# Probabilities over A's rows turned by a crossbar transpose, as two float16 pieces, ahead of the product with A

## The reference, cut to what matters

```python
xn = layernorm(x)                                   # x: (16, 512, 256) float32
# attention: 16 heads of 16, one key and value head for all
q = (xn @ Wq.T + bq) / 4 ; k, v = split(xn @ Wkv.T + bkv)
o = softmax(q k^T) v ; attn = o @ Wo.T + bo
# mixture over E = 6 experts, each with L = 100 low-rank tokens (A: 6x100x16, B: 6x16x256)
gates = one_hot(argmax(xn @ w_gate))                # TOP_K = 1: the chosen gate is 1
tokens = A @ B
p = softmax(xn . tokens / sqrt(C))                  # over the 100 rows of A, per expert
val = tokens @ wt_w.T + wt_b
delta_f = p[:, 1:] @ val[1:]                        # row 0 is left out
delta = ((delta_f + xn) @ wd_w.T + wd_b) * scale
out = x + attn + xn + log(sum_e gates_e * exp(delta_e))
```

## Time and profile before

| what | us |
|---|---|
| median of 3 runs | 902.43 (899.44 to 903.38) |
| the profiled execution, its own time | 902.32 |
| its span, first to last instruction | 900.4 |
| TensorE busy | 857.9 |
| VectorE busy | 780.2 |
| ScalarE busy | 674.6 |
| GpSimd busy | 512.7 |

### The profile page before, as it was taken

The page is one execution under the profiler, slowest core; times in us unless marked ns, Lnnn a source line. Parts: engine busy times, 40 slices in busy tenths (PEclk is TensorE's granted clock), DMA queues, the critical chain, the costliest instruction groups (busy, mean ns, idle before and its releaser), DMA issues.

```text
span 900.4 us, 17856 instructions
## 1 busy us (share of the span) xinstructions
PE 857.9 (95%) x5913; PEld 288.0 (32%) x5913; DVE 780.2 (87%) x1489; ACT 674.6 (75%) x1370; POOL 512.7 (57%) x691
## 2 busy tenths in 40 slices
...
DMA packets 125073, 86.06 MB, mean 96 GB/s; under 512 B 57143, under 2 KB 109112, under 8 KB 124984
## 3 DMA queue, kind: packets, MB, share of 16 engines
q1 hardware_dynamic: 124824, 84.82, 38.2%
q10 hardware_dynamic: 160, 0.10, 0.0%
...
## 4 chain that ended last, share of the span: by engine, by line
PE 79%; DVE 15%; issue 3%; ACT 1%; POOL 1%; DMA 1%; SPq 0%; DVEq 0%
PE pO L373 25%; PE pA L355 19%; DVE M L829 9%; PE pB L360 8%; PE pA L496 5%; PE pA L443 5%; PE pA L514 4%; PE pA L498 3%; PE pA L432 2%; PE pA L468 2%; PE pA L483 2%; DVE st L749 2%; PE pB L476 1%; ACT P L648 1%; PE pB L454 1%
## 5 line engine op out<-in xcount | busy, mean ns | idle before, releaser
L829 DVE TENSOR_REDUCE M<-pA 128x1 f32<-128x512 f32 x1024 | 651.9, 681 | 80.1 <-PE pA L355 76.0
L648 ACT ACTIVATE P<-pB 128x512 f32<-128x512 f32 x1002 | 555.4, 603 | 133.2 <-PE pB L360 129.6
L355 PE MATMUL pA<-K,Q 48*128 48x512 f16 x1024 | 324.6, 388 | 25.1 <-DVE M L829 9.8
L360 PE MATMUL pB<-Q,K 50*128 50x512 f16 x1002 | 317.5, 385 | 0.3 <-DVE M L829 0.3
L373 PE MATMUL pO<-P,VK 128*32 128x512 f32 x2048 | 273.5, 606 | 2.1 <-ACT OTr L654 1.1
L355 PEld LDWEIGHTS pA<-K,Q 48*128 48x128 f16 x1024 | 67.8, 94 | 344.7 <-DVE M L829 285.1
L975 POOL TENSOR_SCALAR Cz<-Cx 128x512 f32<-128x512 f32 x32 | 62.1, 1941 | 38.6 <-ACT Cx L630 38.6
L373 PEld LDWEIGHTS pO<-P,VK 128*32 128x32 f32 x2048 | 40.5, 108 | 99.2 <-issue 66.2
L514 PE MATMUL pA<-wo,On 128*128 128x256 f32 x246 | 70.2, 407 | 0.0
L360 PEld LDWEIGHTS pB<-Q,K 50*128 50x128 f16 x1002 | 64.0, 94 | 7.4 <-ACT P L648 5.5
L960 POOL TENSOR_SCALAR Ms<-M 128x32 f32<-128x32 f32 x32 | 9.7, 303 | 97.5 <-DVE M L829 97.5
...
## 6 DMA issues: line engine op xcount, KB each, us to landing
o_parts<-OTr SPq DMA_DIRECT2D x62, 256.0 KB, 2.3
...
out<-OUT SPq DMA_DIRECT2D x32, 256.0 KB, 3.4
Op<-o_parts SPq DMA_DIRECT2D x31, 256.0 KB
Rb<-l_parts SPq DMA_DIRECT2D x31, 256.0 KB
Q<-q_pieces SPq DMA_DIRECT2D x30, 256.0 KB, 4.5
...
```

Of the source, the lines that this page charges most:

```text
L355: e.matmul(bank1("ab", t)[:, :], Q16[r:r + 48, b % 3, h, 128 * s:128 * s + 128], K16[r:r + 48, b % 3, :], start=True, stop=True).then_inc( ...
L360: e.matmul(bankB(t)[:, :], K16[r:r + 50, b % 3, 128 * i:128 * i + 128], Q16[r:r + 50, b % 3, :, 32 * hh:32 * hh + 32], start=True, stop=Tr ...
L648: e.activation(P[:, u % PR, :], bankB(u + LB)[:, :], ACT.Exp, scale=alpha).then_inc(S("e"))
L829: e.tensor_reduce(M[:, t // 32 % 2, t % 2, t % 32 // 2:t % 32 // 2 + 1], bank1("ab", t)[:, :], AX, ALU.max, negate=True).then_inc(S("mx"))
```

## The change

- The float32 transposes "p" on TensorE and the copy "pte" on ScalarE go. GpSimd, behind En in "snorm", writes En as two float16 pieces (a cast, then a subtraction) into EP, 128 x 2 x 4 x 128 with zeros in the last 28 columns of each block.
- A new step "pd" at 51 modulo 64 on SyncE's queue: one crossbar transpose of EP, 8 blocks of 128x128, into PT. It waits for the low piece and for the product of the batch before.
- "a" becomes three float16 matmuls of 512 columns over the pieces of A and of the probabilities. A's pieces are made once, in the new step "ams" on GpSimd, scaled by the power of two of the weights; A counts in that power, so it is loaded early, from ScalarE's queue, and its maximum joins the setup of VectorE.
- The sums of the softmax are scaled by 2^-11 ahead of the reciprocal (one more VectorE operation of 128x4 per batch); "mm" takes the scale back through a scalar operand.
- Order: "a" moves from 59 to 63 modulo 64, d0 from 63 to 3, d1 from 3 to 7; o0 moves from 7 to 31, o1 from 31 to 35, o2 from 35 to 51 (a batch's o0 is at 159 in place of 135, o2 at 179 in place of 163); position 59 of TensorE is empty. guard0, dlog0, radd0, residual, qs0, qw0, ks, kd, qs1, qw1, guard1, dlog1, radd1 and the second half's lr, or, rec, lw, rb, on move later by 1.2 to 5 tiles. The second lr and or now stand behind pd (52.8 and 52.9 against 51), and the second rb (62.4) behind xtd (61.8).

The diff, cut to its core (fac gains an eighth factor, 2^-33 times the weights' power, copied with the others):

```diff
@@ -38,20 +38,20 @@
 SLOT = {
     "load": -116, "stats0": -97, "stats1": -96, "stats2": -95, "stats3": -94, "aggr": -93, "var": -92.4,
     "root": -91.4, "refine": -90.2, "norm": -87.2, "ph": -82.4, "pl": -79, "xtd": -66.2,
-    "residual": 9.1, "q0": -53, "qe0": -51.4, "qs0": -47.5, "qw0": -45, "uk": -49, "uke": -47.4, "ks": -45.2,
-    "kd": -42.6, "vg": -45, "vge": -44.3, "q1": -41, "qe1": -39.4, "qs1": -38.2, "qw1": -35.6,
+    "residual": 12.8, "q0": -53, "qe0": -51.4, "qs0": -43.8, "qw0": -41.4, "uk": -49, "uke": -47.4, "ks": -41.5,
+    "kd": -38.8, "vg": -45, "vge": -44.3, "q1": -41, "qe1": -39.4, "qs1": -37, "qw1": -34.4,
     "vt": -37, "vte": -36.4, "gate": -34.8, "mask": -32.6, "mkd": -31.4,
     "qread": -25.8, "utm": -24.9, "s": -21,
-    "smax": -20.4, "sexp": -18.8, "ssum": -17.4, "snorm": -16.2, "p": -13, "pte": -12.4, "a": -5, "mm": -4.4,
-    "d0": -1, "dexp0": -0.4, "d1": 3, "dexp1": 3.6, "guard0": 4.8, "dlog0": 9.4, "radd0": 14.8,
-    "d2": 39, "dexp2": 39.6, "d3": 47, "dexp3": 47.6, "guard1": 51.7, "dlog1": 56.2, "radd1": 57.6,
-    "o0": 135, "fo0": 135.6, "o1": 159, "fo1": 159.6, "st0": 163.2, "o2": 163, "fo2": 163.6, "o3": 183,
+    "smax": -20.4, "sexp": -18.8, "ssum": -17.4, "snorm": -16.2, "pd": -13, "a": -1, "mm": -0.4,
+    "d0": 3, "dexp0": 3.6, "d1": 7, "dexp1": 7.6, "guard0": 8.8, "dlog0": 14.2, "radd0": 18.5,
+    "d2": 39, "dexp2": 39.6, "d3": 47, "dexp3": 47.6, "guard1": 53.4, "dlog1": 60.2, "radd1": 61.6,
+    "o0": 159, "fo0": 159.6, "o1": 163, "fo1": 163.6, "st0": 165.2, "o2": 179, "fo2": 179.6, "o3": 183,
     "fo3": 183.6, "st1": 188.6,
 }
...
-    "utm": -30, "s": 9, "smax": 9.6, "sexp": 10.2, "ssum": 10.8, "snorm": 11.4, "p": 17, "pte": 17.6, "a": 21, "mm": 21.6,
+    "utm": -30, "s": 9, "smax": 9.6, "sexp": 10.2, "ssum": 10.8, "snorm": 11.4, "pd": 12.6, "a": 21, "mm": 21.6,
...
-LAST_BUT_ONE = {"o3": 171, "fo3": 171.6, "st1": 172.2}
+LAST_BUT_ONE = {"o2": 167, "fo2": 167.6, "o3": 171, "fo3": 171.6, "st1": 172.2}
...
-    "bs": -86, "scl": -85.8, "xl1": -85.6, "wh": -85.4, "wl": -85.2, "alpha": -60, "warm0": -89, "warm1": -85.9, "qra": -53.5, "qrb": -38, "wdh": -35, "scd": -35,
+    "bs": -86, "scl": -85.8, "xl1": -85.6, "wh": -85.4, "wl": -85.2, "alpha": -60, "ams": -30, "warm0": -89, "warm1": -85.9, "qra": -53.5, "qrb": -38, "wdh": -35, "scd": -35,
...
-PARTH = {"lr": (82.2, 114.2), "or": (82.3, 114.3), "rec": (88.8, 120.8), "lw": (89.6, 121.4), "rb": (92.4, 124.4),
-         "on": (98.2, 130.3)}
+PARTH = {"lr": (82.2, 116.8), "or": (82.3, 116.9), "rec": (88.8, 122.8), "lw": (89.6, 123.4), "rb": (92.4, 126.4),
+         "on": (98.2, 132.3)}
...
-        PT = sb("PT", [128, T])
+        EP = sb("EP", [128, 2, 4, 128], F16)
+        PT = sb("PT", [128, 2, 4, 128], F16)
+        AmP = sb("AmP", [128, 2, ER + 1], F16)
+        asc = sb("asc", [128, 1])
...
-        amx = sb("amx", [128, 1])
+        amx = sb("amx", [128, 2])
...
-            "vt": lambda b: (S("gt"), b + 1), "p": lambda b: (S("pte"), b + 1),
+            "vt": lambda b: (S("gt"), b + 1), 
...
-                if (b := due("p", n)) is not None:
-                    w.wait_ge(*before2("p", b))
-                    w.wait_ge(S("en"), b + 1)
-                    for i in range(4):
-                        mm = e.transpose(bank2("p", b)[0:NL, 128 * i:128 * i + 128], En[:, i, :], idf[:, :])
-                    mm.then_inc(S("pt"))
-
                 if (b := due("a", n)) is not None:
                     w.wait_ge(*before1("a", b))
-                    w.wait_ge(S("pte"), b + 1)
-                    w.wait_ge(S("am"), 16)
-                    e.matmul(bank1("a", b)[0:ER + 1, :], Am_s[0:NL, :], PT[0:NL, :],
-                             start=True, stop=True).then_inc(S("ma"))
+                    w.wait_ge(S("ptd"), 16 * (b + 1))
+                    w.wait_ge(S("amp"), 2)
+                    for k, (ap, pp) in enumerate(PIECES):
+                        mm = e.matmul(bank1("a", b)[0:ER + 1, :], AmP[0:NL, ap, :], PT[0:NL, pp, :, :],
+                                      start=(k == 0), stop=(k == 2))
+                    mm.then_inc(S("ma"))
...
+            w.wait_ge(S("am0"), 1)
+            e.dma_start(Am_s[1:NL, 0:ER], Am[1:NL, :]).then_inc(S("am"), 16)
...
-                if (b := due("pte", n)) is not None:
-                    w.wait_ge(S("pt"), b + 1)
-                    w.wait_ge(S("ma"), b)
-                    e.copy(PT[0:NL, :], bank2("p", b)[0:NL, :]).then_inc(S("pte"))
...
-                    w.wait_ge(S("wm"), 6)
-                    e.tensor_tensor(wmx[:, 2:3], amx[:, :], wmx[:, 0:1], ALU.max).then_inc(S("wm"))
+                    e.memset(amx[:, 1:2], 0.0).then_inc(S("am3"))
+                    w.wait_ge(S("am"), 16)
+                    w.wait_ge(S("am3"), 1)
+                    e.tensor_reduce(amx[0:NL, 1:2], Am_s[0:NL, 0:ER], AX, ALU.max,
+                                    apply_absolute_value=True).then_inc(S("wm"))
                     w.wait_ge(S("wm"), 7)
+                    e.scalar_tensor_tensor(out=wmx[:, 2:3], in0=amx[:, 0:1], scalar=amx[:, 1:2], in1=wmx[:, 0:1],
+                                           op0=ALU.max, op1=ALU.max).then_inc(S("wm"))
+                    w.wait_ge(S("wm"), 8)
                     e.scalar_tensor_tensor(out=rng[:, :], in0=wmx[:, :], scalar=float(C), in1=bmx[:, :],
...
-                    w.wait_ge(S("t0"), 7)
+                    e.tensor_scalar(fac[:, 7:8], two[:, 2:3], 2.0 ** -33, None, ALU.mult).then_inc(S("t0"))
+                    w.wait_ge(S("t0"), 8)
...
                     e.tensor_reduce(sL[:, :], Es[:, :, :], AX, ALU.add).then_inc(S("sl"))
                     w.wait_ge(S("sl"), b + 1)
                     w.wait_ge(S("en"), b)
+                    e.tensor_scalar(sL[:, :], sL[:, :], 2.0 ** -11, None, ALU.mult).then_inc(S("sl2"))
+                    w.wait_ge(S("sl2"), b + 1)
                     e.reciprocal(sR[:, :], sL[:, :]).then_inc(S("sr"))
...
+                    w.wait_ge(S("asc"), 3)
                     w.wait_ge(S("d"), 4 * b)
-                    e.tensor_tensor(MmT[0:ER + 1, :], bank1("a", b)[0:ER + 1, :], mkT[0:ER + 1, :],
-                                    ALU.mult).then_inc(S("mm"))
+                    e.scalar_tensor_tensor(out=MmT[0:ER + 1, :], in0=bank1("a", b)[0:ER + 1, :], scalar=asc[0:ER + 1, 0:1],
+                                           in1=mkT[0:ER + 1, :], op0=ALU.mult, op1=ALU.mult).then_inc(S("mm"))
...
+            e.memset(EP[:, :, :, :], 0.0).then_inc(S("ep0"))
...
                 if (b := due("snorm", n)) is not None:
                     w.wait_ge(S("sr"), b + 1)
-                    w.wait_ge(S("pt"), b)
                     e.tensor_tensor(En[:, :, :], Es[:, :, :], bc(sR[:, :], NL), ALU.mult).then_inc(S("en"))
+                    w.wait_ge(S("en"), b + 1)
+                    w.wait_ge(S("ptd"), 16 * b)
+                    w.wait_ge(S("ep0"), 1)
+                    e.tensor_copy(EP[:, 0, :, 0:NL], En[:, :, :]).then_inc(S("eh"))
+                    w.wait_ge(S("eh"), b + 1)
+                    e.tensor_tensor(EP[:, 1, :, 0:NL], En[:, :, :], EP[:, 0, :, 0:NL], ALU.subtract).then_inc(S("el"))
+
+                if due("ams", n) is not None:
+                    w.wait_ge(S("scl"), 1)
+                    w.wait_ge(S("am"), 16)
+                    w.wait_ge(S("amd"), 1)
+                    e.memset(asc[:, :], 2.0 ** -11).then_inc(S("asc"))
+                    w.wait_ge(S("asc"), 1)
+                    e.tensor_copy(asc[0:ER, :], scl[0:ER, 7:8]).then_inc(S("asc"))
+                    e.tensor_scalar(Am_s[0:NL, 0:ER], Am_s[0:NL, 0:ER], scl[0:NL, 3:4], None, ALU.mult).then_inc(S("asc"))
+                    w.wait_ge(S("asc"), 3)
+                    e.tensor_copy(AmP[0:NL, 0, :], Am_s[0:NL, :]).then_inc(S("amp"))
+                    w.wait_ge(S("amp"), 1)
+                    e.tensor_tensor(AmP[0:NL, 1, :], Am_s[0:NL, :], AmP[0:NL, 0, :], ALU.subtract).then_inc(S("amp"))
...
-            w.wait_ge(S("am0"), 1)
-            e.dma_start(Am_s[1:NL, 0:ER], Am[1:NL, :]).then_inc(S("am"), 16)
...
+                if (b := due("pd", n)) is not None:
+                    w.wait_ge(S("el"), b + 1)
+                    w.wait_ge(S("ma"), b)
+                    e.dma_start_transpose(PT[:, :, :, :].rearrange("p k i t -> p (k i) t"),
+                                          EP[:, :, :, :].rearrange("p k i n -> p (k i n)")).then_inc(S("ptd"), 16)
```

More of the change, by code:

```diff
@@ L80 @@
 QUARTER = {"ot": 63.3, "ow": 64.2}
-PARTH = {"lr": (82.2, 114.2), "or": (82.3, 114.3), "rec": (88.8, 120.8), "lw": (89.6, 121.4), "rb": (92.4, 124.4),
-         "on": (98.2, 130.3)}
+PARTH = {"lr": (82.2, 116.8), "or": (82.3, 116.9), "rec": (88.8, 122.8), "lw": (89.6, 123.4), "rb": (92.4, 126.4),
+         "on": (98.2, 132.3)}
 PARTH_LAST = {"lr": 86.2, "or": 86.3, "rec": 88.8, "lw": 89.4, "rb": 92.2, "on": 98.3}
```

(10 more changed lines are left out.)

4 lines of the change are left out of this document (2 added, 2 removed).

## The result

The changed kernel takes 902.71 us (median of 20 runs, 900.57 to 903.87), the kernel before, run beside it on the same chip, 900.50 (20 runs, 898.99 to 903.38). The ratio is 1.0018, 95% interval 1.0009 to 1.0026: some 2 us more, small but clear of the noise, where 15.7 us less were forecast, and outside the forecast range of 880 to 899. The profiled execution took 903.14 us, its span 901.4, against 902.32 and 900.4.

What follows compares the result with a forecast made beforehand. TensorE, busy 95% of the span, was taken as the bound. Thirteen middle periods at 1.05 us gave -13.7; with setup, first and last batches the total was -15.7, from 902.3 to 886.6, said as 887 us; range 880 to 899.

Steps and rivals of the forecast that it cites:

- TensorE, taken away: TensorE: four transposes (0.67) go, float32 product (1.04) becomes three float16 matmuls (0.70); relief 1.01 us a batch.
- The cuts with a forecast length: Four-tile stretches: tiles 4 to 7 at 3.27, 48 to 51 about 3.18, 52 to 55 at 3.14 us.
- Tiles 56 to 63: Stretch with the empty slot: 6.52 becomes 5.20 us, -1.32, including 0.34 to 0.37 of new wait.
- One light-slot wait takes the place of another: Middle batch: why the 1.05 us gain taken agrees with the 1.01 of TensorE work removed.
- ScalarE, "isn't the bound, so 0": ScalarE: the copy of the turned probabilities goes, counted as 0 us a batch.
- SP and GpSimd, 0: SP's queue and GpSimd: added cast, subtraction, transpose and moved steps cost 0 us a batch.
- GpSimd or SP hands the gain back: Rival: a late guard makes ScalarE wait at dlog0 or dlog1; with 1 us lost a batch, 901 us; chance 0.08.
- The read of totals: SP's read lands 0.6 us before its reciprocal, cost 0; rival: VectorE's reciprocal waits for it, 907 us, chance 0.09.
- The transpose: SP: issue some 2 us, landing 4.3, over 3 us spare; rival: late, stopping TensorE, 905 us, chance 0.03.
- VectorE becomes the bound: Rival: VectorE limits around slot 59, 896 us, chance 0.14; sign: VectorE without idle in tiles 48 to 63.
- Ends: Outside middle batches: setup +0.3, batch 0 -1.5, batch 1 -0.7, last batch +0.9, behind it -1.0 us.

Runs made afterwards that it cites:

- the filled slot: Kernel of run 5 with two idle matmuls of 512 float16 columns in the empty TensorE slot 59: 899.29 us, ratio 0.9978.
- run 2: Changed kernel with dlog0 at 16.2 in place of 14.2: 901.91 us, ratio 1.0014.
- product at 59: Kernel of run 5 with the product back at 59, d0 at 63 and d1 at 3, slot 7 empty: 891.14 us, ratio 0.9889.
- run 1: Changed kernel with batch 0's residual put back at 9.1, as before the change: 898.99 us, ratio 0.9978.
- run 5: Changed kernel with dlog0 at 16.2 and batch 0's transpose at 11.9 in place of 12.6, ahead of the load of batch 2: 898.58 us, ratio 0.9974.
- experiment 6: Load of x moved from slot -116 to -111.5, behind the o parts' write: on run 5's kernel 894.96 us, ratio 0.9926; on product at 59, 891.00 us.

## Why the prediction was wrong, step by step

- *TensorE, taken away* (1.01 a batch): right, its busy time fell by 1.05. By the slots it is 0.67 + 0.26 = 0.93, since the three matmuls cost 0.78, not 0.70, a small miss. The cuts with a forecast length came within 0.01 of it, but for the one below.
- *Tiles 56 to 63* (5.20): the mechanism was right, the second half of the pair waits for the first exponential, but it cost 0.51 where I had 0.34, and 0.08 is the product. Measured 5.45. "One light-slot wait takes the place of another" holds; the filled slot shows that half a microsecond of the empty slot is no gain at all.
- *ScalarE, "isn't the bound, so 0"*: this step failed in the period. It is busy only 80% of a batch, yet the exponential that TensorE needs next stands behind odd jobs in its order. Each moved step of ScalarE had to be laid beside the copy of the o parts and the slot's length on TensorE: dlog0 at 14.2 cost 0.21 a batch (run 2), and d0 moved away from slot 63 cost 0.22 at tile 0, where its 1.2 us had covered the copy (product at 59). Together with the 0.25 above that is 0.68 of the 1.05, 13 times.
- *SP and GpSimd, 0*: this failed in batch 0 and in single batches. I listed the residual among the moved steps and counted its place on GpSimd alone; the load of x waits for it on SP, and in batch 0 the new transpose is queued behind that load, where I had counted no slack: +3.75 instead of -1.5, of which 3.3 went with the residual back (run 1) or 4.3 with the transpose ahead (run 5). The same late load, now 1.0 us ahead of a write of the o parts, came with a later landing of that write and cost 1.1 us in two batches; with the order turned round none stood out (experiment 6). My rival "GpSimd or SP hands the gain back" named the wrong waiter, the guard; it was the logarithm of the variance.
- *The read of totals*: right. "DVE Rc <- DMA" shows once, as before. The rival fell.
- *The transpose*: right that it isn't late, and the estimates were too high: issue 1.26 for 2, landing 3.1 for 4.3. The Trainium skill (VectorE: DVE Perf Modes, The three transpose paths) gives 1309 ns for one 128x128 block on this path; here eight land 3.1 us after the issue, and taking the whole transpose away moved the period by 0.01. No run has the float16 product with the transposes on TensorE, so the two ways are not compared by themselves; the 0.67 that TensorE's transposes took is the price of the other one.
- *VectorE becomes the bound*: fell, though its sign showed in part: in the changed kernel VectorE is busy for the whole of tiles 52 to 55 and 60 to 63 (3.14 of 3.14, 3.47 of 3.47). The first cut has the length of its TensorE jobs, and in the second TensorE waits for ScalarE (the count of the tiles above). With the product at 59 VectorE has 47.17 of work in 51.60 and is full in tiles 60 to 63 (3.27 of 3.27), yet this cut has the length of its TensorE jobs.
- *Ends*: the last batch (+0.9) was exact, batch 1 (-0.59) and the tail (-0.75) near.

So the removed work was real, and most of it can be had: the product at 59, dlog0 at 16.2 and the transpose ahead of the load take 891.1 us, 9.5 less than the kernel before, and beat both. By the profiles (spans of 889.4 and 900.4) 4.7 us are still missing against the forecast: 3.4 in the period (0.80 for 1.05 a batch), 1.8 in batch 0 and 0.9 in the setup, less 1.5 that batch 1 and the last batch give.
